# A graph layer's gather: iterations of 64 tiles, one tile of which SyncE loads row by row

## What is computed

```python
h = relu(layernorm(x))
s, v = (h[:, :32] @ W_up_s) / sqrt(32), einsum(h[:, 32:], W_up_v) / sqrt(32)
w0, w1, w2, w3 = split(silu(silu(edge_feats @ A1 + b1) @ A2 + b2) @ A3, 4)
ss, vs = s[sender], v[sender]
out_s0, out_s3 = ss * y_s * w0, einsum(vs, y_v) / sqrt(3) * w3
out_v1, out_v2 = ss * y_v * w1, vs * y_s * w2
message = segment_sum(concat(out_s0, out_s3, out_v1, out_v2), receiver) / 10
x + message @ (W_out_s, W_out_v) / 8
```

## Time and profile before

| | us |
|---|---|
| median of 3 runs | 1956.28 |
| lowest, highest run | 1956.12, 1959.0 |
| the profiled execution, its own time | 1956.74 |
| its span, first to last instruction | 1954.4 |
| mean granted TensorE clock (share of full speed) | 0.962 |

### The profile page before, as it was taken

The page is one execution under the profiler, slowest core; times in us unless marked ns, Lnnn a source line. Parts: engine busy times, 40 slices in busy tenths (PEclk is TensorE's granted clock), DMA queues, the critical chain, the costliest instruction groups (busy, mean ns, idle before and its releaser), DMA issues.

```text
span 1954.4 us, 58819 instructions
## 1 busy us (share of the span) xinstructions
PE 1837.3 (94%) x20902; PEld 1374.6 (70%) x20902; DVE 1339.3 (69%) x2623; ACT 437.6 (22%) x836; POOL 1445.9 (74%) x1580
## 2 busy tenths in 40 slices
PE   6999999999999999999999999999999999999995
PEld 4677677767776777677777767776777677777773
DVE  5777667766766777676766766676667667766773
ACT  3222212221212222222222221222122222222221
POOL 4777777777777777777777777777777777777774
PEclk8999999999999999999999999999999999999997
DMA  8222222222222222222222222222222222222222
GB/s 238 61 62 58 62 59 61 59 62 58 61 58 62 59 61 59 61 60 59 61 60 61 59 62 59 61 58 62 60 61 58 62 58 61 59 63 59 61 61 101
DMA packets 116918, 128.39 MB, mean 66 GB/s; under 512 B 70818, under 2 KB 89794, under 8 KB 116772
## 3 DMA queue, kind: packets, MB, share of 16 engines
q0 software_dynamic: 48800, 99.49, 20.5%
q1 hardware_dynamic: 67524, 28.62, 5.7%
q10 hardware_dynamic: 576, 0.05, 0.0%
HBM read 121.61 MB, written 6.43 MB: 66 GB/s over the span
## 4 chain that ended last, share of the span: by engine, by line
POOL 68%; issue 24%; PE 3%; DMA 1%; POOLq 1%; DVE 1%; SPq 1%; DVEq 0%; ACT 0%; ACTq 0%
POOL rows L559 68%; PE pss L822 1%; DMA x_sb<-in_x 1%; DMA rows<-node_table,src_in 1%; POOLq L554 1%; PE psw L789 1%; PE pss L811 1%; POOLq L556 0%; POOLq L564 0%; DVE msgs L709 0%; SPq L264 0%; PE ps L773 0%; PE ps L779 0%; SPq L254 0%; DMA node_table<-tab_sb 0%
## 5 line engine op out<-in xcount | busy, mean ns | idle before, releaser
L559 POOL DMA_INDIRECT rows<-node_table,src_in x1515 | 1430.0, 944 | 471.9 <-issue 471.0
L822 PEld LDWEIGHTS pss<-tab_sb,x_sb 128*128 128x128 f32 x4704 | 590.8, 201 | 83.1 <-issue 63.0
L822 PE MATMUL pss<-tab_sb,x_sb 128*128 128x128 f32 x4704 | 620.0, 288 | 0.0
L789 PE MATMUL psw<-a_bd,h 128*128 128x256 f32 x1568 | 437.4, 403 | 3.5
L707 DVE TENSOR_TENSOR msgs<-rows,psw 128x256 f32<-128x256 f32 x392 | 165.1, 421 | 333.8 <-DMA rows<-node_table,src_in 314.6
L685 DVE TENSOR_TENSOR x_sb<-picks_in,psx 128x1024 f32<-128x1024 int32 (+1 forms) x294 | 363.5, 1238 | 34.0 <-PE pss L822 33.5
L811 PE MATMUL pss<-msgs,onehot 128*32 128x64 f32 (+1 forms) x12544 | 306.0, 239 | 79.1 <-DVE msgs L709 78.5
L709 DVE TENSOR_TENSOR msgs<-rows,psw 128x768 f32<-128x768 f32 x392 | 371.2, 947 | 0.0
L811 PEld LDWEIGHTS pss<-msgs,onehot 128*32 128x32 f32 x12544 | 241.0, 112 | 173.9 <-DVE msgs L709 117.9
L594 ACT ACTIVATE h<-ps,b_sb 128x512 f32<-128x512 f32 x196 | 134.7, 687 | 875.1 <-PE ps L779 875.1
L789 PEld LDWEIGHTS psw<-a_bd,h 128*128 128x128 f32 x1568 | 274.1, 195 | 52.0 <-issue 12.1
(11 more groups left out here) (67 smaller groups left out, 386.3 us busy)
## 6 DMA issues: line engine op xcount, KB each, us to landing
rows<-node_table,src_in POOLq DMA_INDIRECT x1515
ef_in<-in_efT SPq DMA_DIRECT2D x98, 64.0 KB
picks_in<-in_picks SPq DMA_DIRECT2D x50, 64.0 KB
xT_sb<-in_xT SPq DMA_DIRECT2D x7, 448.0 KB, 8.3
x_sb<-in_x SPq DMA_DIRECT2D x7, 448.0 KB, 7.5
attr_in<-in_attr SPq DMA_DIRECT2D x98, 32.0 KB
out_T<-xT_sb SPq DMA_DIRECT2D x1, 3136.0 KB, 8.8
node_table<-tab_sb SPq DMA_DIRECT2D x7, 256.0 KB, 3.8
```

What stands on the lines that cost most here:

```text
L559: pool.indirect_dma_start(out=rows[:, QT * p + t, :], out_offset=None, in_=table, in_offset=bass.IndirectOffsetOnAxis(ap=src_in[:, b, at:a ...
L789: last = nc.tensor.matmul(psw[:, p % SLOTS, 2 * i:2 * i + 2].rearrange("p b c d e -> p (b c d e)"), h2[:, b, h, (2 * half + i) * P:(2 * ha ...
L822: last = nc.tensor.matmul(pss[:, o % 2, CH:CH + F], pick[:, t, :], tab_sb[:, t, :], start=False, stop=(p % 2 == 1 and t == PICK_BLOCKS[p + ...
```

## The change

An iteration is four blocks: 16 quads, 64 tiles (`BODY = 4`). The arrays are padded to 100 blocks; the last iteration still handles 98 blocks' worth, that is 8 quads, with its own bounds (`LAST_QUADS`, `LAST_OCTS`), so 24 full iterations and a short one replace 48 full and a short one. Row slots, message slots, one-hots and h2 keep their number and are used twice per iteration (`RING` = 8 quads). Two of the 64 tiles are computed on PE, as before (one per 8 quads). One more, the last tile of quad 15, isn't gathered by POOL: SP loads its 128 rows with 128 DMAs of one row each (512 bytes), the node numbers taken from a list in SBUF into registers, 32 at a time. The rows go into a slot of their own (`SINGLE_SLOT`, the 33rd), and quad 15 takes slots 29 to 32 instead of 28 to 31.

SP issues these rows in four parts with the block loads between them. Before the first part it waits for the list and for the last message of the iteration before (`claim_singles`). `messages` of quad 15 waits on four more semaphores. The loads for block b of the next iteration stand behind part b + 1 of the rows, the first pick list behind parts 1 to 3. In the prologue SP loads the senders of four blocks instead of two, and before the loop those of the list and of blocks 2 and 3 as well.

The core of the diff:

```diff
@@ -41,18 +41,26 @@
-BODY = 2
+BODY = 4
-NJ = -(-N_EDGES // (BLOCK * BODY))
-NB = NJ * BODY
+NB = -(-N_EDGES // (BLOCK * 2)) * 2
+NJ = -(-NB // BODY)
+NBP = NJ * BODY
+LAST_QUADS = (NB - (NJ - 1) * BODY) * QUADS
+RING = 2 * QUADS
+HBUF = 2
-PICK_SLOT = QT * QB - 1
+PICK_SLOT = QT * RING - 1
+SINGLE_SLOT = PICK_SLOT + 1
+SINGLE_PART = P // BODY
+PICKS = QB // RING
...
 def quad_gathers(p):
 
-    return QT - 1 if QT * (p + 1) - 1 == PICK_SLOT else QT
-
-
+    if p == QB - 1:
+        return QT - 2
+    return QT - 1 if p % RING == RING - 1 else QT
+
+
+def quad_slot(p):
+
+    return QT * (p % RING) + (1 if p == QB - 1 else 0)
...
+                    def load_list(j):
+                        sp.dma_start(list_in[:, :], singles[bass.ds(j, 1), :]).then_inc(list_loaded, 16)
+
+                    def claim_singles(j):
+
+                        sp.wait_ge(list_loaded, j * 16 + 16)
+                        sp.sem_inc(singles_claimed, 1)
+                        sp.wait_ge(msgs_ready, j * QB + MSG_CREDIT)
+                        sp.sem_inc(singles_claimed, 1)
+
+                    def gather_singles(b):
+
+                        e0 = b * SINGLE_PART
+                        nodes = nc.values_load_multi_w_load_instructions(
+                            list_in[0:1, e0:e0 + SINGLE_PART], engines=[mybir.EngineType.SP], min_val=0, max_val=NPAD - 1,
+                            skip_runtime_bounds_check_because="the senders are node numbers")[1]
+                        for e, node in enumerate(nodes, e0):
+                            sp.dma_start(rows[e:e + 1, SINGLE_SLOT, :], table[bass.ds(node, 1), :]
+                                         ).then_inc(singles_gathered[b], 16)
+
+                    def load_block(j, b):
+
+                        last_quad = b * QUADS + QUADS - 1
+                        sp.wait_ge(gathered[last_quad], j * 16 * quad_gathers(last_quad) + 16 * quad_gathers(last_quad))
+                        load_src(j + 1, b)
+                        sp.wait_ge(l1_done, j * OCTS + 2 * b + 2)
+                        load_ef(j + 1, b)
+                        sp.wait_ge(onehot_ready, j * OCTS + 2 * b + 2)
+                        load_attr(j + 1, b)
+
+                    def next_picks(j, i):
+
+                        sp.wait_ge(pick_ready, (j * PICKS + i + 2) * PICK_STEPS)
+                        load_picks(j * PICKS + i + 2)
...
                     sp.wait_ge(pick_ready, PICK_STEPS)
                     load_picks(1)
+                    sp.wait_ge(table_stored, 16 * NCH * len(PIECES))
                     with sp.Fori(0, NJ - 1) as j:
+                        claim_singles(j)
                         for b in range(BODY):
-                            last_quad = b * QUADS + QUADS - 1
-                            sp.wait_ge(gathered[last_quad], j * 16 * quad_gathers(last_quad) + 16 * quad_gathers(last_quad))
-                            load_src(j + 1, b)
-                            sp.wait_ge(l1_done, j * 2 * BODY + 2 * b + 2)
-                            load_ef(j + 1, b)
-                            sp.wait_ge(onehot_ready, j * 2 * BODY + 2 * b + 2)
-                            load_attr(j + 1, b)
-                        sp.wait_ge(pick_ready, j * PICK_STEPS + 2 * PICK_STEPS)
-                        load_picks(j + 2)
+                            gather_singles(b)
+                            if b == BODY - 1:
+                                load_list(j + 1)
+                            if b > 0:
+                                load_block(j, b - 1)
+                            if b == RING // QUADS:
+                                next_picks(j, 0)
+                        load_block(j, BODY - 1)
+                        next_picks(j, 1)
+                    sp.wait_ge(list_loaded, 16 * NJ)
+                    sp.wait_ge(picks_loaded, 16 * NJ * PICKS)
...
@@ -557,7 +620,7 @@
                         for t in range(tiles):
                             at = QT * k + t
                             pool.indirect_dma_start(
-                                out=rows[:, QT * p + t, :], out_offset=None, in_=table,
+                                out=rows[:, quad_slot(p) + t, :], out_offset=None, in_=table,
```

```diff
...
-                    def messages(j, p, tiles):
+                    def messages(j, p, tiles, singles):

                         dve.wait_ge(gathered[p], j * 16 * quad_gathers(p) + 16 * tiles)
+                        if singles:
+                            for b in range(BODY):
+                                dve.wait_ge(singles_gathered[b], j * 16 * SINGLE_PART + 16 * SINGLE_PART)
...
+                            half, r = divmod(p, RING)
...
+                            if not last and 1 <= r <= PICK_STEPS:
+                                dve.wait_ge(pick_used, (j * PICKS + half) * PICK_STEPS + r)
+                                pick_blocks(j * PICKS + half + 1, r - 1)
```

More of the change, by code:

```diff
@@ L145, in gnn_layer_kernel @@
         rstd = sb("rstd", [P, NT])
-        rows = sb("rows", [P, QT * QB, F])
+        rows = sb("rows", [P, SINGLE_SLOT + 1, F])
         msgs = sb("msgs", [P, MSG_SLOTS, QT, 2, F])
@@ L217, in gnn_layer_kernel @@
         src_again = sem("src_again")
+        list_loaded = sem("list_loaded")
+        singles_claimed = sem("singles_claimed")
+        singles_gathered = [sem(f"singles_gathered{b}") for b in range(BODY)]
         picks_loaded = sem("picks_loaded")
@@ L566, in _ @@
                             gather(j, p, quad_gathers(p))
-                    for p in range(QB):
+                    for p in range(LAST_QUADS):
                         gather(NJ - 1, p, quad_tiles(p))
@@ L612, in iteration @@
                     def iteration(j, first=False, last=False):
-                        for o in range(OCTS):
+                        for o in range(LAST_OCTS if last else OCTS):
                             ahead = (j, o + 2) if o + 2 < OCTS else (j + 1, o + 2 - OCTS)
@@ L617, in iteration @@
                                 copy_sums(j, o - 1, not last)
-                            if not (last and o + 2 >= OCTS):
+                            if not (last and o + 2 >= LAST_OCTS):
                                 silu_1(*ahead)
@@ L727, in iteration @@
                     def iteration(j, first=False, last=False):
-                        for p in range(QB):
+                        for p in range(LAST_QUADS if last else QB):
                             g = p // 2 + 1
-                            ahead = (j + g // 4, g % 4) if not (last and 2 * g >= QB) else None
+                            half, r = divmod(p, RING)
+                            ahead = (j + g // OCTS, g % OCTS) if not (last and 2 * g >= LAST_QUADS) else None
                             n = 2 * p - WINDOW_LAG
@@ L736, in iteration @@
                                     add_window(j, n + i)
[L737 to L742 removed]
+                            if not last and r in (RING - 3, RING - 1):
+                                place_picked(j, half, (r - RING + 3) // 2)
+                            messages(j, p, quad_tiles(p) if last else quad_gathers(p), not last and p == QB - 1)
+                            if not last and 1 <= r <= PICK_STEPS:
+                                dve.wait_ge(pick_used, (j * PICKS + half) * PICK_STEPS + r)
+                                pick_blocks(j * PICKS + half + 1, r - 1)
                             if ahead and p % 2 == 0:
@@ L757, in _ @@
                     iteration(NJ - 1, last=True)
-                    for n in range(2 * QB - WINDOW_LAG, 2 * QB):
+                    for n in range(2 * LAST_QUADS - WINDOW_LAG, 2 * LAST_QUADS):
                         add_window(NJ - 1, n)
@@ L845, in iteration @@
                     def iteration(j, first=False, last=False):
-                        for p in range(QB):
+                        for p in range(LAST_QUADS if last else QB):
                             o, half = divmod(p, 2)
                             ahead = (j, o + 2) if o + 2 < OCTS else (j + 1, o + 2 - OCTS)
-                            if p + 1 < QB:
+                            if p + 1 < (LAST_QUADS if last else QB):
                                 layer_3(j, p + 1)
@@ L860, in iteration @@
                                 scatter(j, p)
-                            if not last and p < PICK_STEPS:
+                            if not last and p % RING < PICK_STEPS:
                                 pick_rows(j, p)
```

83 lines of the change are left out of this document (44 added, 39 removed).

## The result

| | before | after |
|---|---|---|
| median, us | 1957.38 (6 runs, 1956.12 to 1959.23) | 2142.68 (6 runs, 2140.74 to 2144.14) |
| span of the profiled execution, us | 1954.4 | 2140.6 |
| mean granted TensorE clock | 0.962 | 0.899 |

The changed kernel takes 1.0946 times as long (95% interval 1.0934 to 1.0958), 185 us more. The forecast was 30 us less.

What follows compares the result with a forecast made beforehand. POOL's gathers were taken to bound the kernel: 1956.7 us less 30.0 for 24 gathers plus 0.9 for the prologue made 1927.6, given as 1927.5. The range was 1924 to 1936 us, the full range up to 2200.

Steps and rivals of the forecast that it cites:

- POOL's gain: POOL's gathers: 61 instead of 62 per 64 tiles, 24 fewer at 1.249 us each, 30.0 us saved.
- the 0.9 charged: SP's prologue: four loads of senders instead of two before the first loads, +0.9 us.
- Where the change can fail: SP in the loop: 128 one-row loads and four register loads per 64 tiles could delay quad 9's pick list.
- The formula: DVE at quad 9: list lands after 7.2 + 0.75 K; the wait is made up while 0.75 K + 32.3 is under 76.2.
- K: SP's rows plus register loads per 64 tiles: 56.5 us, ends 49.8 and 100, to stay under 58.5.
- I take 0.41: SP's issue of one row in the loop: 0.41 us, from 0.38 to 0.48; 128 rows make 52.5 us.
- I take 1.0 us for each of the four: SP's loads of 32 registers, four per 64 tiles: 1.0 us each, 4.0 us together.
- 27.2 x 71.5 / 77.4 = 25.1 us at PE's pace: PE from quad 9's first pick block to the iteration's last message: 25.1 us, against 27.2 at POOL's pace.
- rival 4: SP's loop body no longer fits and is fetched each turn at 1.7 us: 1928 to 1935 us; chance 0.04.
- Rival 1: SP's four loads of 32 registers go word by word, 8 us each: about 2395 us; chance 0.28.
- Rival 2: SP's rows cost what loads with 128 partitions do, 0.48 us each: 2051 us; chance 0.18.
- Rival 3: PE's 74.23 us are true need, so DVE's 0.6 us stalls are not made up: 1942 us; chance 0.06.

## Why the prediction was wrong

**POOL's gain was right.** 24 gathers went, at 1.249 us each. The version with the early list and the hints takes 76.19 us per 64 tiles (76.2 forecast) and gains 26.6 of the 29.1 us net that the sum had (24 to 30 by its interval). The prologue's first gather moved from 42.81 to 43.20 us, 0.4 us for the 0.9 charged.

**Where the change can fail was right too:** SP in the loop, through the pick list for quad 9. The formula held in form, but four of its terms were mis-sized. The list was to come after 0.2 + 0.75 K + 4.4 + 0.6 + 2 us, and 25.1 us were to follow.

| from the last message of an iteration | forecast | measured |
|---|---|---|
| claim, with SP's turn | 0.2 | 1.9 |
| three quarters of K | 42.4 | 46.4 |
| two blocks and the list's issue | 5.0 | 5.1 |
| flight | 2.0 | 3.0 |
| sum: first pick block of quad 9 | 49.6 | 56.4 |
| from there to the last message at PE's pace | 25.1 | 29.0 |
| iteration, if this is longer than POOL's 76.2 | 74.7 | 85.4 |

*The first failed step is K*, "I take 0.41" and "I take 1.0 us for each of the four": a row is 0.425 us and a register load 2.06. The register load is the larger miss, 4.2 of the 6.1 us; the row was right within 4%, and by itself that is 1.9 us. The chosen values left 2.0 us for everything, and the text called this its thinnest point. The range of K, 49.8 to 100, was right; to put most of the chance at its low end was not borne out by a row, since no row had shown a load of more than one register. The Trainium skill ("Runtime: NRT & Kernel Launch", section Instruction fetch mechanics) gives about 200 ns per register even in bulk, by which 32 would take 6.4 us, an estimate. The trace does not agree: 2.06 us for 32, and 0.053 us for each register more.

*The second failed step is what follows the list*, and it counts for as much. "27.2 x 71.5 / 77.4 = 25.1 us at PE's pace" spreads PE's lead over POOL evenly over the iteration. It isn't even: the pairs of quads with pick blocks take PE 9.80 us and the pair without them 6.36, and what follows the list is mostly pairs with pick blocks. In the kernel without rows PE, never idle and at a granted clock of 1.00, takes 28.28 us for it. With 28.3 in the place of 25.1 the limit of K is (76.2 - 7.2 - 28.3) / 0.75 = 54.3 us, not 58.5, so that the forecast's own K of 56.5 was over it: the formula then gives 77.9 us an iteration and no gain. Even the shortest such stretch in the traces, 27.1 us in the run with 29 loads a part, puts the limit at 55.9. In the changed kernel the stretch is 29.2 us in the mean of 23 iterations. The 0.9 us above the kernel without rows fit the wait, in which PE runs dry and behind which its clock is 0.50: a late list costs a little more than its lateness.

That K alone was not the fault shows in both directions. With K at its measured 62.6 and all else as forecast the formula gives 0.75 x 62.6 + 32.3 = 79.3 us an iteration, 24 x 3.1 = 74 us above the forecast or about 2001 us, where 2142.68 was measured. With K at 57.5 it has 76 us, and the run with 29 loads a part took 80.6 by POOL's counter.

*The third is the turn, and beside it the flight.* The flight was taken from a list of 8 KB and is 3.0 us for the broadcast pick list. On the turn, rival 4, "the loop's body no longer fits", had 0.04, and looked at SP alone with 1.7 us. SP pauses 3.0 to 3.4 us, of which only what lies behind the last message counts (1.9 us instead of 0.2); the hints are worth 46.6 us in the kernel with the late list, mostly this. On PE, at which I did not look, the branch grew from 0.215 to 3.64 us. That one is hidden behind SP while the list is late (2144.95 without it) and is worth 37 to 43 us once the list is early. Here the rule of the Trainium skill (the same page and section: a taken branch whose target is outside the engine's two-page window waits for a fetch) agrees with the traces: 215 packets on one instruction queue, and 10 to 17 as soon as PE's loop alone is short or hinted. I had read in 18 packets that no loop fetches itself anew, and not asked which engine's body would double to what size.

**The rivals.** Rival 1 (registers word by word, from 1.5 us a load on) is nearest: the load is 2.06 us, over its point of decision, though not the 8 us it was priced with. Rival 2's mechanism, rows at 0.45 to 0.48, fell: 0.425. Rival 3 fell in the version with hints, where PE's work does not hold POOL up.

**Why 185 us.** Two edits in a row divide it: the moved load is worth 168 us, then the hints 43, nearly all of it PE's turn, and what is left is POOL's gain of 26.6: 168 + 43 - 26.6 = 184. By the ratios, each against its own chip, it is 173 + 39 - 27 = 185.

## What to carry to other kernels

Slack that an engine has over a whole iteration need not be spread evenly over it: the limit is to be worked out for the stretch in which the delay has to be made up. When an idle queue is given work, look at what else stands on it: the load that another engine waits for is to be placed by when it is wanted, ahead of the filler, and one line decided 168 us here. A loop body that grows is to be read per engine at its turn (the duration of the branch, the packets of the instruction queues), and a hint on the back edge or a shorter loop on that engine removes the pause. A cost of which the trace has only a one-element case should be taken near the middle of its bounds when the plan survives only its low end.

## What the runs showed of the hardware

- A register load on SP from SBUF took 0.78 us for 8 registers and 2.06 for 32, so 0.053 us for each register and, if the cost is linear, 0.36 us once.
- A load of one row of 512 bytes with its address from a register occupies SP's queue for 0.225 us, and one follows the next after 0.425 us (0.418 with hints).
- At the turn of the loop of 64 tiles PE stood 3.5 to 3.7 us, SP 3.0 to 3.4 and DVE 1.5, where PE's loop of 32 tiles had a branch of 0.21 us. With the hints it was gone on each: PE's branch went from 3.64 to 0.216 us, SP's pause from 3.4 to 0.2, and the packets from 215 and 262 to 17 and 13.
- After PE had stood 3.5 us at its turn the next 5 us had a granted clock of 0.50 to 0.52, and the 5 us behind them 0.70 to 0.79.
